# Walsh-Hadamard transform of a ternary feed-forward layer: one butterfly stage moved from VectorE into TensorE's Hadamard products

## The chip, the cores and the metric

The kernel runs as one program on one core of a Trainium2 chip. The metric is the device time of one execution in microseconds (us). In the profile PE is TensorE (PEld its weight loads), DVE is VectorE, ACT is ScalarE, POOL is GpSimd and SP is SyncE, which only issues transfers here. A line such as L1541 is a line of the kernel before.

## The reference, cut to what matters

Two decoder layers of six blocks, each followed by a residual sum and a layer norm, on x of 4 x 512 x 512. Only the third block is touched, a feed-forward block with ternary weights and 8-bit activations, with a Walsh-Hadamard transform ahead of its last product:

```python
def fwht(x):                      # over the last dimension, n = 2048
    h = 1
    while h < n:
        x = x.reshape(-1, n // (2 * h), 2, h)
        a, b = (x[..., 0, :], x[..., 1, :])
        x = jnp.stack([a + b, a - b], axis=-2).reshape(-1, n)
        h *= 2
    return x * (1.0 / np.sqrt(n))

gate = bitlinear(x, w_gate)       # (4, 512, 512) -> (4, 512, 2048)
up = bitlinear(x, w_up)
intermediate = jax.nn.silu(gate) * up
return h_bitlinear(intermediate, w_down)   # act_quant(fwht(.)), then 2048 -> 512
```

The transform of 2048 numbers has eleven stages. Seven act inside blocks of 128 numbers, and are a product with a 128 x 128 matrix of +1 and -1. Four act between the sixteen blocks: distance 1, 2, 4 and 8 blocks.

## The kernel before, in words

The function `ternary_ffn` holds the block. Its work is cut into 16 tiles of 128 rows, and each engine runs its own in-order program, written out by hand as `step(t)` for t from -1 to 15, with semaphores between them. In step t, TensorE makes the gate and up products of tile t in four chunks of 512 columns (`gate_up`, L1511: 8 products of 128x512 bf16 each), turns the rounded transform of tile t-3 (`turn_y`, L1521), turns the butterflied z of tile t-2 (`turn_z`, L1531), multiplies it by the Hadamard matrix (`products`, L1541: four blocks to a PSUM bank, sixteen in all), turns the quantized input of tile t+1 (`turn_q`, L980) and makes the down product of tile t-3 (`down`, L1555). The order is: gate_up 0 and 1, turn_y, turn_z, gate_up 2, products, gate_up 3, turn_q, down. The turned tiles and the products share banks 5 to 7 in rotation; a bank is taken again when ScalarE has copied it out.

VectorE in step t multiplies silu(gate) by up, chunk by chunk (`z_chunk`, L1376, into z), makes three butterfly stages of tile t-1 (`butterfly_stage` 0, 1, 2: distance 2, 4, 8 blocks, each one addition and one subtraction of 128x1024, L1185 and L1186), the quantization of tile t+1, the peaks of |y| of tile t-2 (`peaks`, L1397 to L1406), the residual sum and statistics of tile t-3, and the rounding of y of tile t-2 (`round_y`, L1423). Its order is: z_chunk 0, stage 0, z_chunk 1, stage 1, z_chunk 2, quantized, stage 2, z_chunk 3, peaks, add_down (L1413), statistics, round_y, scale. GpSimd makes the remaining stage, distance 1, from z into z1 (also L1185 and L1186, after the four chunks of z). The stages then go z1 to z2, z2 to z1, z1 to z2, and `turn_z` reads z2.

ScalarE makes the silu (L1276), and copies the turned z (`keep_zT`, L1298), the products (`keep_y`, L1308) and the turned y (`keep_yT`, L1288) out of PSUM. Between peaks and round_y it scales y and adds the rounding constant (`shift_y`, L1314). So the chain of one tile is: products, keep_y, peaks, shift_y, round_y, turn_y, down. In steps 2 and 3 VectorE also rounds the last four chunks of the down weights, and ScalarE copies them to their home (`weights.keep`, L620) ahead of the first `down`.

The Hadamard matrix (`had`, 64 KB) is loaded by SyncE in the stage before. After step 15 the rest of the tiles is worked off: on TensorE turn_y(13), turn_z(14), down(13), products(14), turn_z(15), the first projection of the next block (L92), products(15), turn_y(14), the second projection, down(14), turn_y(15), down(15).

## Time and profile before

| | us |
|---|---|
| median of three runs | 1766.6 |
| lowest and highest run | 1761.59, 1771.72 |
| the profiled execution, whole | 1760.69 |
| its span in the trace | 1758.8 |
| PE busy in the span | 1591.5 |
| DVE busy | 1296.5 |
| ACT busy | 936.4 |
| POOL busy | 690.9 |

A row of groups or of the timeline gives where an instruction starts, how long its record is, and the idle time of its engine before it with the instruction that ended that idle time. A record of a matmul includes its run through the array, which the next one overlaps, so the distance between two starts tells what a matmul costs, and the record does not. The touched block lies between about 504 and 837 us of the span.

### The profile page before, as it was taken

What the parts mean: (1) busy time and instruction counts of PE and PEld (TensorE: products, weight loads), DVE (VectorE), ACT (ScalarE), POOL (GpSimd) and SP (SyncE); (2) the same over time, 40 slices, a digit from 0 to 9 for tenths busy, and PEclk for the clock granted to TensorE, in tenths of its full rate; (3) what the DMA queues carried; (4) which work ended last, traced back from release to release, by engine and by line L of the source; (5) the groups of instructions that cost most, each with busy time, mean ns of one, the idle gap of its engine ahead of it and who ended that gap; (6) DMA issues with size and microseconds to landing.
All of it is one profiled execution on the core that took longest, in us unless ns stands there. A gap on an engine that the chain in (4) does not pass through costs nothing. (4 is left out here: it accounts for less than half of the span.)

```text
span 1758.8 us, 26394 instructions
## 1 busy us (share of the span) xinstructions
PE 1591.5 (90%) x8780; PEld 1121.4 (64%) x8812; DVE 1296.5 (74%) x2354; ACT 936.4 (53%) x1932; POOL 690.9 (39%) x646
## 2 busy tenths in 40 slices
PE   7999998999867899999889999999898989999995
PEld 5788875555525556566666566565566767677774
DVE  6466656666888899997687585784849999767574
ACT  3221226776665566666566465473634555555542
POOL 5034265776522332323332222322132235555553
PEclk9999999999988999999999999999999999999998
DMA  6200018533020000003312121121233100000000
GB/s 213 75 1 24 1 49 234 173 97 97 26 96 1 1 1 1 1 1 104 89 55 73 37 73 55 55 73 37 86 99 93 46 10 1 1 25 12 13 24 24
DMA packets 66849, 95.72 MB, mean 54 GB/s; under 512 B 12176, under 2 KB 28688, under 8 KB 66716
## 3 DMA queue, kind: packets, MB, share of 16 engines
q1 hardware_dynamic: 58460, 80.40, 15.0%
q0 software_dynamic: 6144, 12.60, 2.8%
q8 instruction: 72, 1.18, 0.3%
q10 hardware_dynamic: 2112, 1.05, 0.2%
q14 instruction: 61, 0.50, 0.1%
HBM read 56.25 MB, written 4.19 MB: 34 GB/s over the span
## 5 line engine op out<-in xcount | busy, mean ns | idle before, releaser
L2948 PE MATMUL bank<-fp_xT,fp_weights_values 128*128 128x512 f32 x704 | 187.1, 404 | 11.6 <-DVE fp_gate L2851 9.8
L1783 ACT ACTIVATE causal_probs<-bank,causal_neg 128x512 f32<-128x512 f32 (+3 forms) x256 | 134.1, 530 | 106.0 <-DVE causal_neg L1853 70.8
L2948 PEld LDWEIGHTS bank<-fp_xT,fp_weights_values 128*128 128x128 f32 x704 | 129.7, 190 | 57.1 <-DVE fp_gate L2851 18.0
L2975 PE MATMUL bank<-fp_wd,fp_hT 128*128 128x512 f32 x528 | 133.8, 394 | 4.6 <-DVE X L2873 3.4
L2860 DVE SCALAR_TENSOR_TENSOR fp_up<-bank,fp_weights_scales,fp_up 128x512 f32<-128x512 f32 x132 | 99.1, 751 | 44.5 <-ACT fp_up L2758 37.0
L820 DVE TENSOR_REDUCE heads_neg<-bank 128x1 f32<-128x512 f32 x128 | 86.7, 679 | 57.7 <-PE bank L869 57.6
L782 ACT ACTIVATE heads_probs<-bank,heads_neg 128x512 f32<-128x512 f32 x128 | 88.1, 689 | 77.1 <-DVE heads_neg L820 77.1
L1126 POOL DMA_DIRECT2D causal_qS<-causal_qk x96 | 48.4, 511 | 202.3 <-DVE causal_qk L1118 202.2
L1185 POOL TENSOR_TENSOR ternary_z<-ternary_z 128x1024 f32<-128x1024 f32 x16 | 37.7, 2354 | 206.1 <-DVE ternary_z L1376 206.1
L2975 PEld LDWEIGHTS bank<-fp_wd,fp_hT 128*128 128x128 f32 x528 | 98.5, 188 | 28.9 <-issue 6.6
L1511 PE MATMUL bank<-weights_raw,ternary_qT 128*128 128x512 bf16 x433 | 104.7, 388 | 4.6 <-DVE ternary_z L1376 2.6
L2020 PE MATMUL bank<-eye,causal_probs 128*128 128x128 f32 x640 | 101.8, 283 | 5.2 <-ACT causal_pT L1765 3.7
L92 PE MATMUL bank<-rope_xT,rope_wT 128*128 128x512 f32 x384 | 93.6, 402 | 10.7 <-DVE rope_wT L420 10.7
L2009 PE MATMUL bank<-causal_kS,causal_qS 96*128 96x512 f32 (+3 forms) x256 | 84.5, 382 | 20.0 <-ACT causal_probs L1783 17.2
L330 POOL TENSOR_TENSOR rope_qk<-rope_rot 128x512 f32<-128x512 f32 x32 | 43.0, 1343 | 145.4 <-DVE rope_rot L433 143.9
L80 PE MATMUL bank<-eye,heads_probs 128*128 128x128 f32 x512 | 77.8, 275 | 21.5 <-ACT heads_pT L790 21.4
L2731 POOL TENSOR_TENSOR fp_gate<-fp_gate 128x512 f32<-128x512 f32 x44 | 56.9, 1293 | 100.4 <-DVE fp_gate L2851 100.4
L2752 ACT ACTIVATE fp_gate<-bank,fp_weights_scales 128x512 f32<-128x512 f32 x88 | 60.0, 686 | 62.1 <-PE bank L2948 56.1
L2020 PEld LDWEIGHTS bank<-eye,causal_probs 128*128 128x128 f32 x640 | 78.0, 145 | 22.9 <-issue 12.7
L80 PEld LDWEIGHTS bank<-eye,heads_probs 128*128 128x128 f32 x512 | 59.8, 141 | 51.2 <-ACT heads_probs L782 39.6
L92 PEld LDWEIGHTS bank<-rope_xT,rope_wT 128*128 128x128 f32 x384 | 73.0, 192 | 28.0 <-DVE rope_xT L415 10.7
L2851 DVE SCALAR_TENSOR_TENSOR fp_gate<-bank,fp_weights_scales,fp_gate 128x512 f32<-128x512 f32 x88 | 63.7, 747 | 29.7 <-ACT fp_gate L2752 29.3
(266 smaller groups left out, 4128.2 us busy)
## 6 DMA issues: line engine op xcount, KB each, us to landing
pairs_xd<-X SPq DMA_DIRECT2D x64, 128.0 KB, 2.7
pairs_cd<-in_ctx SPq DMA_DIRECT2D x64, 128.0 KB, 2.8
causal_qS<-causal_qk SPq DMA_DIRECT2D x96, 64.0 KB, 2.8
causal_qS<-causal_qk POOLq DMA_DIRECT2D x96, 64.0 KB, 2.5
causal_kS<-causal_qk SPq DMA_DIRECT2D x96, 64.0 KB, 2.7
causal_kS<-causal_qk POOLq DMA_DIRECT2D x96, 64.0 KB, 2.5
X<-in_x SPq DMA_DIRECT2D x4, 1024.0 KB, 7.8
heads_cT<-in_ctxT SPq DMA_DIRECT2D x4, 1024.0 KB, 6.1
```

Of the source, the lines that this page charges most:

```text
L80: last = pe.transpose(bank[:, k * P:(k + 1) * P], source[:, k, :], ident)
L92: last = pe.matmul(bank, lhs(a, k), rhs(c, k), start=n == 0, stop=n == len(steps) - 1)
L782: act.activation(probs[:, n % 4], banks[n % 3][:], ACT.Exp, bias=neg[:, g % 2, k:k + 1], accum_out=total[:, g % 2, k:k + 1]).then_inc(prob ...
L820: dve.tensor_reduce(neg[:, g % 2, k:k + 1], banks[n % 3][:], AX, ALU.max, negate=True).then_inc(neg_ready, 1)
L1511: last = pe.matmul(to[:], qT[:, t % 2, k], w[c][:, k], start=k == 0, stop=k == NF - 1)
L1783: act.activation(probs_of(i)[:, h + one], view[:, one], ACT.Exp, bias=neg[:, G % 2, at:at + 1], accum_out=total[:, G % 2, at:at + 1]).then ...
L2009: last = pe.matmul(view[:, one], qS[0:3 * DH, G % 2, h + one, i * P:(i + 1) * P], kS[0:3 * DH, G % 2, h + one, 0:(i + 1) * P], start=True, ...
L2020: last = pe.transpose(banks[3 + n % 2][:, h * P:(h + 1) * P], probs_of(i)[:, h, j * P:(j + 1) * P], ident)
L2851: dve.scalar_tensor_tensor(out=part, in0=banks[4 + g][:], scalar=scale(n, g, 0), in1=part, op0=ALU.mult, op1=ALU.add).then_inc(gate_odd, 1)
L2860: dve.scalar_tensor_tensor(out=up[:, n % 2], in0=banks[4 + g][:], scalar=scale(n, g, 1), in1=up[:, n % 2], op0=ALU.mult, op1=ALU.add).then ...
L2948: last = pe.matmul(banks[4 + g][:], values[:, g, n % NI, of], xT[:, part, g], start=part == 0, stop=part == 1)
L2975: last = pe.matmul(banks[t][:], hT[:, n % SLOTS, a, t * P:(t + 1) * P], wd[:, c, i], start=i == 0 and k == 0, stop=i == NI - 1 and k == 2)
```

## The change

The stage of distance 1 leaves the vector engines. TensorE makes it in the Hadamard products: for two neighbouring blocks a and b of the turned z, and the matrix H, the pair of results is [aH + bH, aH - bH]. Where each of the sixteen blocks was multiplied by H alone (128 columns), the first block of a pair is now multiplied by [H, H] (`both`, H read twice) and the second by [H, -H] into the same 256 columns of PSUM, the second accumulating on the first. GpSimd's stage becomes distance 2, VectorE's two stages distance 4 and 8, and its third is gone. The result of the butterflies lies in z1 instead of z2, so `turn_z` reads z1, and GpSimd, which writes z1, waits for `z_turned` of two tiles before in place of the butterflies; VectorE's wait for `z_turned` goes. The matrix in DRAM holds H and -H (128 KB); it has its place in this block, is loaded by SyncE at the block's begin, ahead of the last two loads of weights, and TensorE waits for it ahead of products(0).

```diff
@@ SyncE, stage before
-            start.load_hadamard(sp)
@@ ternary_ffn
+        had = m.sbuf("had", [P, 2, P])
+        both = had[:, 0:1].to_broadcast([P, 2, P])
...
             past.over(sp)
+            sp.dma_start(had[:], hadamard).then_inc(had_loaded, 16)
...
                 pool.wait_ge(z_ready, CH * (t + 1))
                 if t >= 2:
-                    pool.wait_ge(butterfly, 3 * (t - 1))
-                butterflies(pool, z[:, t % 2], z1[:, t % 2], 1).then_inc(first_done, 1)
+                    pool.wait_ge(z_turned, CH * (t - 1))
+                butterflies(pool, z[:, t % 2], z1[:, t % 2], 2).then_inc(first_done, 1)
...
-                src, dst = (z1, z2) if n % 2 == 0 else (z2, z1)
+                src, dst = (z1, z2) if n == 0 else (z2, z1)
                 if n == 0:
                     dve.wait_ge(first_done, t + 1)
-                    if t >= 2:
-                        dve.wait_ge(z_turned, CH * (t - 1))
                 else:
-                    dve.wait_ge(butterfly, 3 * t + n)
-                butterflies(dve, src[:, t % 2], dst[:, t % 2], 2 << n).then_inc(butterfly, 1)
+                    dve.wait_ge(butterfly, 2 * t + 1)
+                butterflies(dve, src[:, t % 2], dst[:, t % 2], 4 << n).then_inc(butterfly, 1)
...
                     quantized(t + 1)
-                butterfly_stage(t - 1, 2)
...
-            for n in range(3):
+            for n in range(2):
                 butterfly_stage(LAST, n)
...
-                    for k in range(4):
-                        last = pe.matmul(to[:, k * P:(k + 1) * P], zT[:, 4 * c + k], had[:], start=True, stop=True)
+                    for k in (0, 2):
+                        pair = to[:, k * P:(k + 2) * P].rearrange("p (two n) -> p two n", two=2)
+                        pe.matmul(pair, zT[:, 4 * c + k], both, start=True, stop=False)
+                        last = pe.matmul(pair, zT[:, 4 * c + k + 1], had[:], start=False, stop=True)
                     last.then_inc(y_ready, 1)
...
-        "hadamard": hadamard(P),
+        "hadamard": np.stack([hadamard(P), -hadamard(P)], axis=1),
```

On TensorE, a step in the middle of the block stands like this before: turn_y (L1521), turn_z (L1531), gate_up 2, the sixteen products, gate_up 3, turn_q, down.

```order
L1521 MATMUL bank<-ternary_eye_2277,ternary_yq 128x128 x16
L1531 MATMUL bank<-eye,ternary_z 128x128 x16
L1511 MATMUL bank<-weights_raw,ternary_qT 128x512 x8
L1541 MATMUL bank<-ternary_had,ternary_zT 128x128 x16
L1511 MATMUL bank<-weights_raw,ternary_qT 128x512 x8
L980 MATMUL bank<-ternary_eye_2277,ternary_q 128x128 x4
L1555 MATMUL bank<-ternary_w_down,ternary_yT 128x512 x16
```

And the same place now, from turn_y (here L1517) to the second pair of products (L1540 the first block of a pair, L1541 the second):

```order
L1517 MATMUL bank<-ternary_eye_2277,ternary_yq 128x128 x16
L1527 MATMUL bank<-eye,ternary_z 128x128 x16
L1507 MATMUL bank<-weights_raw,ternary_qT 128x512 x8
L1540 MATMUL bank<-ternary_had,ternary_zT 128x256
L1541 MATMUL bank<-ternary_had,ternary_zT 128x256
```

There are sixteen products to a tile as before, eight of each line, each of 256 columns instead of 128; nothing else on TensorE has moved.

On VectorE, the middle of a step stands like this before: stage 0 (rows of four runs of 256), a chunk of z, stage 1, a chunk of z, the quantization (L958 to L972), stage 2, the last chunk of z, the peaks.

```order
L1185 TENSOR_TENSOR ternary_z<-ternary_z 128x2x512
L1186 TENSOR_TENSOR ternary_z<-ternary_z 128x2x512
L1376 SCALAR_TENSOR_TENSOR ternary_z<-bank,ternary_steps,ternary_silu 128x512
L958 TENSOR_REDUCE ternary_peak<-X 128x1
...
L972 TENSOR_SCALAR ternary_q<-ternary_q_2273 128x512
L1185 TENSOR_TENSOR ternary_z<-ternary_z 128x1024
L1186 TENSOR_TENSOR ternary_z<-ternary_z 128x1024
L1376 SCALAR_TENSOR_TENSOR ternary_z<-bank,ternary_steps,ternary_silu 128x512
L1397 TENSOR_REDUCE ternary_peak_y<-ternary_y 128x1
```

And now, from the second stage (here the one with runs of 1024) on:

```order
L1183 TENSOR_TENSOR ternary_z<-ternary_z 128x1024
L1184 TENSOR_TENSOR ternary_z<-ternary_z 128x1024
L1375 SCALAR_TENSOR_TENSOR ternary_z<-bank,ternary_steps,ternary_silu 128x512
L952 TENSOR_REDUCE ternary_peak<-X 128x1
...
L966 TENSOR_SCALAR ternary_q<-ternary_q_2273 128x512
L1375 SCALAR_TENSOR_TENSOR ternary_z<-bank,ternary_steps,ternary_silu 128x512
L1394 TENSOR_REDUCE ternary_peak_y<-ternary_y 128x1
```

The pair of butterflies between the quantization and the last chunk of z is gone, and the last chunk follows the quantization directly.

## Rows read from the trace of the kernel before

**Rows 1.** Busy time by stretch: length, PE, PEld, DVE, ACT, POOL, PEclk, DMA

```profile
520.00:560.00 40.00, 25.87 (x139) 16.87 (x140) 33.41 (x50) 22.42 (x32) 9.34 (x4) 0.84 0.00 1
680.00:720.00 40.00, 38.16 (x258) 25.32 (x261) 38.60 (x64) 24.68 (x35) 12.01 (x6) 1.00 0.01 2
```

**Rows 2.** GpSimd's timeline: the same operation in two neighbouring steps

```profile
687.50 2.36 POOL L1185 TENSOR_TENSOR ternary_z<-ternary_z 128x1024 f32<-128x1024 f32 x1 [12.26 <-DVE ternary_z L1376]
705.78 2.35 POOL L1185 TENSOR_TENSOR ternary_z<-ternary_z 128x1024 f32<-128x1024 f32 x1 [12.26 <-DVE ternary_z L1376]
```

**Rows 3.** Timeline of one step, start and length: TensorE from products to turn_y

```profile
717.20 3.73 PE L1541 MATMUL bank<-ternary_had,ternary_zT 128*128 128x128 f32 x32
720.77 1.89 PE L1511 MATMUL bank<-weights_raw,ternary_qT 128*128 128x512 bf16 x8
...
726.17 1.03 PE L1511 MATMUL bank<-weights_first,ternary_qT 128*128 128x512 bf16 x4
727.03 2.75 PE L1511 MATMUL bank<-weights_raw,ternary_qT 128*128 128x512 bf16 x12
730.11 1.07 PE L1521 MATMUL bank<-ternary_eye,ternary_yq 128*128 128x128 bf16 x16 [0.32 <-DVE ternary_yq L1423]
```

**Rows 4.** The same step: VectorE and ScalarE from stage 2 to the rounding

```profile
722.11 1.22 DVE L1186 TENSOR_TENSOR ternary_z<-ternary_z 128x1024 f32<-128x1024 f32 x1
723.25 0.74 DVE L1376 SCALAR_TENSOR_TENSOR ternary_z<-bank,ternary_steps,ternary_silu 128x512 f32<-128x512 f32 x1
726.79 2.00 ACT L1314 ACTIVATE ternary_y<-ternary_y,ternary_rate_y 128x2048 f32<-128x2048 f32 x1 [3.22 <-DVE ternary_rate_y L1406]
728.83 1.23 DVE L1423 TENSOR_SCALAR ternary_yq<-ternary_y 128x2048 bf16<-128x2048 f32 x1
```

**Rows 5.** Groups of instructions, VectorE, 600 to 780 us: busy, mean ns, idle before

```profile
L1186 DVE TENSOR_TENSOR ternary_z<-ternary_z 128x1024 f32<-128x1024 f32 x30 | 36.6, 1219 | 0.0
L1185 DVE TENSOR_TENSOR ternary_z<-ternary_z 128x1024 f32<-128x1024 f32 x30 | 36.5, 1217 | 0.0
```

**Rows 6.** Waits, 600 to 780 us: us in total, times, longest

```profile
PEld bank L1521 <- DVE ternary_yq L1423: 8.6, 10, 1.2
```

**Rows 7.** Groups of f32 matmuls of the next block by width, 840 to 1060 us

```profile
L2040 PE MATMUL bank<-causal_pT,causal_v 128*32 128x256 f32 x56 | 4.3, 379 | 0.0
...
L2080 PE MATMUL bank<-causal_w_o,causal_v_column 128*128 128x512 f32 x8 | 3.6, 592 | 0.0
...
L2040 PE MATMUL bank<-causal_pT,causal_v 128*32 128x128 f32 x56 | 2.8, 273 | 0.0
```

**Rows 8.** Timeline of steps 2 to 4, TensorE and ScalarE's copies of down weights

```profile
539.47 5.45 PE L1541 MATMUL bank<-ternary_had,ternary_zT 128*128 128x128 f32 x32
549.60 1.91 ACT L620 ACTIVATE ternary_w_down<-weights_raw 128x2048 bf16<-128x2048 f32 x1 [0.24 <-DVE weights_raw L615]
556.34 1.89 PE L1521 MATMUL bank<-ternary_eye,ternary_yq 128*128 128x128 bf16 x16 [5.03 <-DVE ternary_yq L1423]
573.28 1.91 ACT L620 ACTIVATE ternary_w_down<-weights_raw 128x2048 bf16<-128x2048 f32 x1 [0.55 <-DVE weights_raw L615]
575.67 4.53 PE L1555 MATMUL bank<-ternary_w_down,ternary_yT 128*128 128x512 bf16 x15 [7.09 <-issue]
583.50 1.06 PE L1521 MATMUL bank<-ternary_eye,ternary_yq 128*128 128x128 bf16 x16
```

**Rows 9.** Timeline of step 15 and the tail

```profile
784.96 1.07 PE L1521 MATMUL bank<-ternary_eye,ternary_yq 128*128 128x128 bf16 x16 [0.33 <-DVE ternary_yq L1423]
795.88 0.75 DVE L1376 SCALAR_TENSOR_TENSOR ternary_z<-bank,ternary_steps,ternary_silu 128x512 f32<-128x512 f32 x1 [1.57 <-ACT ternary_silu L1276]
802.76 1.07 PE L1521 MATMUL bank<-ternary_eye,ternary_yq 128*128 128x128 bf16 x16 [1.64 <-DVE ternary_yq L1423]
819.53 3.73 PE L1541 MATMUL bank<-ternary_had,ternary_zT 128*128 128x128 f32 x32
830.25 1.06 PE L1521 MATMUL bank<-ternary_eye,ternary_yq 128*128 128x128 bf16 x16
```

More of the change, by code:

```diff
@@ L925, with __init__ @@
     QB = 128.0
-    SIZE = 22 * D - 128
-    def __init__(self, nc, names, weights, hadamard, X, banks, ident):
+    def __init__(self, nc, names, weights, X, banks, ident):
         m = self.m = Memory(nc, None, names, "ternary_start")
@@ L931, in __init__ @@
         self.end = self.begin
-        self.weights, self.hadamard, self.X, self.banks, self.ident = weights, hadamard, X, banks, ident
+        self.weights, self.X, self.banks, self.ident = weights, X, banks, ident
         self.q32, self.q, self.qT = (self.place("q32", [P, D], F32, 4 * D), self.place("q", [P, 2, D], BF16, 4 * D),
@@ L935, in __init__ @@
         self.silu = self.place("silu", [P, 2, D], F32, 8 * D)
-        self.eye16, self.had = self.place("eye16", [P, P], BF16, 2 * P), self.place("had", [P, P], F32, 4 * P)
+        self.eye16 = self.place("eye16", [P, P], BF16, 2 * P)
         self.peak, self.step_x, self.rate = (self.place(n, [P, NT], F32, 32) for n in ("peak", "step_x", "rate"))
         self.steps = self.place("steps", [P, NT, 2], F32, 32)
-        self.had_loaded, self.eye_ready = m.sem("had_loaded"), m.sem("eye_ready")
+        self.eye_ready = m.sem("eye_ready")
         self.peaked, self.stepped, self.inverted, self.rated, self.q_shifted, self.q_ready, self.q_turned, self.qT_ready = (
@@ L948, in room @@
         return m.sbuf("start", [P, self.end - self.begin], U8)
-    def load_hadamard(self, sp):
-        sp.dma_start(self.had[:], self.hadamard).then_inc(self.had_loaded, 16)
     def quantized(self, dve, t):
@@ L1018, in __init__ @@
         self.step_in = self.left("step_in", [P, NT - 1, (NT - 1) * GH])
-        self.end = begin + TernaryStart.SIZE
         self.qS, self.kS = self.left("qS", [P, 2, GH, S], F32R), self.left("kS", [P, 2, GH, S], F32R)
@@ L1138, in masked_above, with ternary_ffn @@
         pool.tensor_copy(self.mask[:], ones).then_inc(self.masks, 1)
-def ternary_ffn(nc, block, names, past, start, then, w_ternary, weights, X, norm_tiles, banks, ident):
+def ternary_ffn(nc, block, names, past, start, then, hadamard, w_ternary, weights, X, norm_tiles, banks, ident):
     FF = 4 * D
@@ L1154, in ternary_ffn @@
         start.room(m)
-        had, eye16, qT, silu, steps = start.had, start.eye16, start.qT, start.silu, start.steps
+        eye16, qT, silu, steps = start.eye16, start.qT, start.silu, start.steps
         z = m.sbuf("z", [P, 2, FF])
@@ L1171, in ternary_ffn @@
         down_home = [w_down[:, 4 * c:4 * c + 4].rearrange("p k n -> p (k n)") for c in range(CH)]
+        had_loaded = m.sem("had_loaded")
         q_turned, qT_ready = start.q_turned, start.qT_ready
@@ L1251, in _ @@
                 norm.root(pool, 0, t - 3)
-            pool.wait_ge(butterfly, 3 * TILES)
+            pool.wait_ge(butterfly, 2 * TILES)
             then.kv_lows(pool, 1)
@@ L1526, in turn_z @@
                     return
-                pe.wait_ge(butterfly, 3 * (t + 1))
+                pe.wait_ge(butterfly, 2 * (t + 1))
                 for g in range(CH):
@@ L1530, in turn_z @@
                     for k in range(4):
-                        last = pe.transpose(to[:, k * P:(k + 1) * P], z2[:, t % 2, (4 * g + k) * P:(4 * g + k + 1) * P], ident)
+                        last = pe.transpose(to[:, k * P:(k + 1) * P], z1[:, t % 2, (4 * g + k) * P:(4 * g + k + 1) * P], ident)
                     last.then_inc(z_turned, 1)
@@ L1536, in products @@
                     return
+                if t == 0:
+                    pe.wait_ge(had_loaded, 16)
                 for c in range(CH):
@@ L1578, in step @@
                 down(t - 3)
-            pe.wait_ge(start.had_loaded, 16)
             for t in range(-1, TILES):
@@ L3049, in decoder_kernel @@
                 ternary_names = names()
-                ternary_start = TernaryStart(nc, ternary_names, weights, i["hadamard"], X, banks, ident)
+                ternary_start = TernaryStart(nc, ternary_names, weights, X, banks, ident)
                 heads = head_attention(nc, block, heads_names, rope, pairs, ternary_start, i["ctxT"], i["gamma"], w_ternary, weights, X, norm_tiles[1], banks, ident)
@@ L3055, in decoder_kernel @@
                 causal_start = CausalStart(nc, causal_names, ternary_start.begin, top, gpsimd_copies, i["wqkv"], i["causal_bias"], X, banks, ident)
-                ternary = ternary_ffn(nc, block, ternary_names, heads, ternary_start, causal_start, w_ternary, weights, X, norm_tiles[0], banks, ident)
+                ternary = ternary_ffn(nc, block, ternary_names, heads, ternary_start, causal_start, i["hadamard"], w_ternary, weights, X, norm_tiles[0], banks, ident)
                 heads.names.close()
```

## The prediction, written before the changed kernel was run

> **What bounds the kernel now.** The change touches one block, some 330 of 1759 us, so I read that stretch alone. First the busy times by stretch: in the middle of the block TensorE is busy 38.2 and VectorE 38.6 of 40 us, at a granted clock of 1.00; before that, in the warm-up, neither is, and the clock is 0.84 [rows 1]. Then the period of a step: GpSimd's first butterfly starts at 687.50 and 705.78, so a step takes 18.28 us, with 12.26 us of waiting on GpSimd, which is therefore nobody's bound [rows 2]. Two engines look full, and the question is how much room each has. VectorE's groups show no idle time ahead of the butterflies, and their instructions follow each other at 1.14 us from start to start (722.11 to 723.25) [rows 4, 5]: it has next to none.
>
> For TensorE the busy share says little, since a record holds the run through the array too; I go by starts. From the products at 717.20 to turn_y at 730.11 it has its work back to back, except that the last gate_up record ends at 729.78 and turn_y starts 0.32 us after it, released by the rounding of y [rows 3]. By the weight loads this wait is 8.6 us over 10 steps, 0.86 each [rows 6]. By starts: 12 records of gate_up take 2.75 us and 4 take 1.03, so each costs 0.215, and the last one ends 0.17 us after its share (1.03 - 4 x 0.215) [rows 3]; TensorE could have gone on at 729.61 and lost 0.50 us. That is the wait I use; 0.32 and 0.86 are its bounds. The remaining gaps of a step stand in turn_z, where ScalarE has to empty banks; the change doesn't touch them. So TensorE's own floor is 18.28 - 0.50 = 17.78 us a step: **both engines are full, and TensorE has half a microsecond, not more**.
>
> **What the edit takes from VectorE.** Two instructions of 1.14 us a step, 2.28 us; its work falls to about 16.0 us a step. It is wanted there only if TensorE can follow.
>
> **What it adds to TensorE.** The products are 32 records a tile (each f32 matmul makes two), 3.73 us with one whole record of 0.27 in it: (3.73 - 0.27)/31 = 0.1115 us each [rows 3, 7], 3.57 us in all, which is also the distance to gate_up 3 (717.20 to 720.77) [rows 3]. Now the same 32 have 256 columns. The nearest rows: f32 records of 256 columns last 379 ns and those of 128 columns 273 ns, 106 ns more [rows 7]; and eight f32 records of 512 columns, 0.592 us long, keep TensorE busy for 3.6 us, (3.6 - 0.592)/7 = 0.430 us each, so 0.215 for 256 columns [rows 7]. The first gives 32 x 0.106 = 3.39, the second 32 x 0.215 - 3.57 = 3.31 us more a tile. I take **3.31**; the accumulation on the first block of a pair and the repeated reading of H have no row here, and I give them nothing, with 0 to 0.1 us a tile as bounds.
>
> A rule speaks against such a sum. The Trainium skill ("TensorE: Matmul & The Clock Gate", Back-to-back issue gap) gives sustained 81 ns for a matmul of 128 columns and 131 ns for one of 512. Interpolated, as an estimate, 256 columns would cost 98 ns, 1.2 times those of 128, and the products would add 0.7 us a tile. This trace doesn't agree: 0.1115 and 0.215 us by the rows above. I keep it as a rival with a small chance.
>
> **Whether the wait goes.** TensorE's wait for the rounding of y hangs on the chain products, last chunk of z, peaks, shift, rounding. The last chunk of z began at 723.25, directly behind stage 2, though gate_up 3 had ended at 722.66 [rows 3, 4]. With stage 2 gone it can start at about 722.75, 0.5 us earlier after gate_up 3, and so can peaks, shift_y (726.79 to 728.79) and round_y (728.83 to 730.06). So turn_y would come 9.34 - 0.5 = 8.84 us after gate_up 3 begins, and TensorE's own work ahead of it takes 729.61 - 720.77 = 8.84. They tie: the wait of 0.50 is gone, and nothing more can be had, since TensorE itself is next. A steady step becomes 18.28 + 3.31 - 0.50 = **21.09 us, 2.81 more** (2.45 if all of 0.86 goes, 3.4 if nothing goes and the accumulation costs). VectorE's gain of 2.28 turns into idle time.
>
> **Warm-up.** In steps 2 and 3 TensorE waits 5.03 us for the rounding of y and 7.09 us for the down weights [rows 8], so there the added columns lie beside other work, but not quite: ScalarE makes the silu of the last chunk, which comes after the products, and only then copies down weights. In step 2 the products (539.47, 5.45 us, partly at the lower clock of 1.2 GHz) grow by some 3.4 us, the two copies move behind them, the second from 549.60-551.5 to about 552.8-554.7, and shift and rounding queue behind it: turn_y(0) at 558.0 instead of 556.34, 1.7 late. In step 3 the same happens once more: the last copy, 573.28-575.2, moves to about 576.1-578.0, and down(0), which waits for it, comes 2.8 us late. So turn_y(1), at 583.50, is 2.8 late. If the shorter idle time keeps the higher clock granted, or copies find room, it is 0.8; at worst 3.5.
>
> **Steady part.** From turn_y at 583.50 to 784.96 there are eleven steps (201.5 us) [rows 8, 9]: 11 x 2.81 = 30.9 us (27.0 to 37.4).
>
> **Step 15 and tail.** In step 15 the last chunk of z waits not for VectorE but for ScalarE's silu (1.57 us idle), so VectorE's relief brings nothing and the whole 3.31 reaches turn_y at 802.76. In the tail its two sets of products (819.53 is the second) both stand ahead of turn_y(15) at 830.25, which shows no wait [rows 9]: 6.62. The chain keep_y, peaks, shift, rounding behind the last set moves with it. Together 9.9 (9.3 to 10.3).
>
> **At nothing.** GpSimd's stage has the same 1024 elements an instruction; its new wait for turn_z of two tiles before ends before the fourth chunk of z does, and it has 12.26 us of idle time to cover it. SyncE's load of H, twice as large, is issued at the block's begin, two steps of work ahead of products(0) at 539.47. The memory behind the block moves by 512 bytes a partition.
>
> **Sum.** 2.8 + 30.9 + 9.9 = 43.6 us. On the profiled execution of 1760.7 this gives 1804.3; the median of the runs is 1766.6, 5.9 above it, so I predict 1766.6 + 43.6 = **1810.2 us**, 2.5% slower. By the bounds: 0.8 + 27.0 + 9.3 = 37.1 to 3.5 + 37.4 + 10.3 = 51.2; from the lowest run 1798.7, from the highest 1822.9.
>
> **Rivals.** (a) *The wait stays.* The chain by way of ScalarE gets no shorter, or a new wait (bank rotation of y, the silu behind shift_y) takes its place: 3.31 in each steady step, 11 x 3.31 + 2.8 + 9.9 = 49.1, 1815.7 us. For it: the tie at 8.84 leaves no margin. Against: the last chunk of z does stand directly behind stage 2.
> (b) *TensorE has room, and VectorE's relief is the result.* TensorE's weight loads are busy only 25.3 of 40 us [rows 1]. If that were the measure, 6.7 us a step were free, the 3.31 would vanish in them, and the step would follow VectorE to 16.0 us: 11 x -2.28 = -25, 1741.6 us. It decides where TensorE's floor is under 16.0 - 3.31 = 12.7 us; by the starts it is 17.8. The Trainium skill ("Trainium Kernel Development and Optimization", Performance Expectations) calls matmul busy time a bad metric and the busy share of LDWEIGHTS a good one. Here the first half agrees and the second misleads: loads wait for columns to stream, and the starts show no hole.
> (c) *The columns are mostly hidden,* the pace of 0.1115 being that of the weight loads and not of the 128 columns. Then a tile adds about 0.7 us, a steady step 0.7 - 0.5 = 0.2, and the sum is 11 x 0.2 + 3 x 0.7 + 0.6 = 5 us, 1771.5. Against it: the f32 rows of 128 and 256 columns differ by 106 ns, 128 columns twice over at 2.4 GHz.
>
> **How the numbers follow.** Forecast 0.80, (a) 0.10, (b) 0.05, (c) 0.05. A change under 0.5% (9 us) can hardly be told from none. Faster is (b), 0.05; same is (c), 0.05; slower is the rest, 0.90. The range takes in the forecast's bounds, the spread of the runs and (a): 1797 to 1822; (b) and (c) lie outside.
>
> **What would show it.** Right: GpSimd's first butterflies 21.1 us apart in the middle of the block; 32 records of about 379 ns for the products, 6.9 us to gate_up 3; VectorE busy about 33 of 40 us there with its idle time ahead of the first chunks of z or the add; no more than 0.1 us in TensorE's wait for the rounding; all else in the span as before. Wrong: a period under 20.7 (columns hidden) or over 21.5 (a new wait on TensorE, which would stand ahead of the products or of turn_y), or a block end moved by more or less than the eleven periods tell, which would put the error in the warm-up or the tail.

## The result, and the profile of the changed kernel

The changed kernel took 1806.8 us (median of four runs, 1806.45 to 1809.54) against 1764.4 us of the kernel before on the same chip (also four runs, 1761.59 to 1771.72): a ratio of 1.023, interval 1.0207 to 1.0258. It is slower by 42.4 us; 43.6 were forecast. The span of its profiled execution is 1804.9 us, 46.1 above the 1758.8 of before, at a granted clock of 0.975.

First the busy times by stretch, columns as in [rows 1], one stretch in the warm-up and one in the middle of the block:

```profile
520.00:560.00 40.00, 28.90 (x147) 18.34 (x146) 31.27 (x48) 23.04 (x34) 9.33 (x4) 0.87 0.00 1
...
680.00:720.00 40.00, 39.03 (x224) 25.03 (x223) 30.44 (x51) 21.93 (x32) 12.36 (x6) 1.00 0.00 1
```

In the middle TensorE is now busy 39.03 of 40 us and VectorE 30.44, where [rows 1] had 38.16 and 38.60: one of the two full engines has been relieved, the other is busy almost without a break. The period by GpSimd's timeline, answering [rows 2]:

```profile
683.79 2.35 POOL L1183 TENSOR_TENSOR ternary_z<-ternary_z 128x1024 f32<-128x1024 f32 x1 [14.73 <-DVE ternary_z L1375]
...
704.91 2.35 POOL L1183 TENSOR_TENSOR ternary_z<-ternary_z 128x1024 f32<-128x1024 f32 x1 [14.73 <-DVE ternary_z L1375]
```

704.91 - 683.79 = 21.12 us a step, 18.28 before; GpSimd waits 14.73 us for a tile, 12.26 before. Now TensorE's timeline of a step, answering [rows 3]. The products appear as pairs of records since two lines issue them in turn; the thirteen pairs that follow are left out.

```profile
710.96 1.07 PE L1517 MATMUL bank<-ternary_eye,ternary_yq 128*128 128x128 bf16 x16
...
714.59 1.89 PE L1507 MATMUL bank<-weights_raw,ternary_qT 128*128 128x512 bf16 x8
716.32 0.59 PE L1540 MATMUL bank<-ternary_had,ternary_zT 128*128 128x256 f32 x2
716.75 0.59 PE L1541 MATMUL bank<-ternary_had,ternary_zT 128*128 128x256 f32 x2
717.18 0.59 PE L1540 MATMUL bank<-ternary_had,ternary_zT 128*128 128x256 f32 x2
...
723.22 1.03 PE L1507 MATMUL bank<-weights_raw,ternary_qT 128*128 128x512 bf16 x4
```

Products from 716.32 to gate_up 3 at 723.22: 6.90 us (3.57 in [rows 3]), and turn_y at 710.96 shows no idle time ahead of it. A pair starts every 0.43 us, so each record of 256 columns costs 0.215 us, although it lasts 0.379 by the groups below. The pair that begins a sum (L1540) and the pair that adds to it (L1541) start the next one equally soon, 0.43 us each. VectorE's timeline of the same step, the chunk that comes after the products:

```profile
704.08 0.75 DVE L1375 SCALAR_TENSOR_TENSOR ternary_z<-bank,ternary_steps,ternary_silu 128x512 f32<-128x512 f32 x1 [4.64 <-PE bank L1507]
704.75 2.27 DVE L1394 TENSOR_REDUCE ternary_peak_y<-ternary_y 128x1 f32<-128x2048 f32 x1
...
709.67 1.23 DVE L1420 TENSOR_SCALAR ternary_yq<-ternary_y 128x2048 bf16<-128x2048 f32 x1
```

This is where VectorE's saving went: it stands idle for 4.64 us a step until TensorE has made gate_up 3. Of these, 2.4 come with the longer step, as the first experiment shows, and the rest is the stage that was taken away. The groups and waits over 620 to 800 us (columns as in [rows 5] and [rows 6]) say the same in total:

```profile
L1541 PE MATMUL bank<-ternary_had,ternary_zT 128*128 128x256 f32 x128 | 38.1, 379 | 0.0
```

```profile
DVE ternary_z L1375 <- PE bank L1507: 41.8, 9, 4.7
...
PEld bank L1517 <- DVE ternary_yq L1420: 3.0, 9, 0.3
```

The records are 379 ns long, twice 128 of them in eight steps; VectorE waits 41.8 us for TensorE in nine steps; TensorE's weight loads wait 0.3 us a step for the rounding of y instead of the 0.86 of [rows 6]. Last, the block's ends on TensorE, answering [rows 8] and [rows 9]:

```profile
555.20 1.24 PE L1517 MATMUL bank<-ternary_eye,ternary_yq 128*128 128x128 bf16 x16 [3.33 <-DVE ternary_yq L1420]
```

```profile
574.86 6.06 PE L1555 MATMUL bank<-ternary_w_down,ternary_yT 128*128 128x512 bf16 x16 [4.59 <-issue]
...
584.21 1.06 PE L1517 MATMUL bank<-ternary_eye,ternary_yq 128*128 128x128 bf16 x16
```

```profile
816.57 1.07 PE L1517 MATMUL bank<-ternary_eye,ternary_yq 128*128 128x128 bf16 x16
...
837.70 1.07 PE L1517 MATMUL bank<-ternary_eye,ternary_yq 128*128 128x128 bf16 x16 [1.64 <-DVE ternary_yq L1420]
...
842.99 5.15 PE L1555 MATMUL bank<-ternary_w_down,ternary_yT 128*128 128x512 bf16 x16
```

The landmarks give the account of the span. "Block start" is GpSimd's last sum of the attention stage (497.41 us before, 498.46 after); "first scores" is TensorE's first matmul of the next block's scores (837.53 and 880.90).

| Stretch | before, us | after, us | difference | forecast |
|---|---|---|---|---|
| start to block start (code unchanged) | 497.41 | 498.46 | +1.05 | 0 |
| block start to turn_y at 583.50 / 584.21 | 86.09 | 85.75 | -0.34 | +2.8 |
| eleven steady steps | 201.46 | 232.36 | +30.90 | +30.9 |
| step 15 | 17.80 | 21.13 | +3.33 | +3.31 |
| tail, to the first scores | 34.77 | 43.20 | +8.43 | +6.6 |
| first scores to the end (code unchanged) | 921.3 | 924.0 | +2.7 | 0 |
| span | 1758.8 | 1804.9 | +46.1 | +43.6 |

The rows of the steps fit. The tail is 1.8 us longer than forecast and the warm-up 3.1 shorter. The two stretches of unchanged code vary by themselves: over the profiled executions of before and of the first four experiments below, the last one takes 921 to 928 us.

### The profile page after: what moved, and what is told of

Same layout as the page of the kernel before. It is cut to its first block and busy times, and to the rows that moved or that the text cites. A ratio compares the mean times of both kernels' runs of the same rounds, so it can differ in the third digit from the quotient of the medians.

```text
span 1804.9 us, 26379 instructions
## 1 busy us (share of the span) xinstructions
PE 1649.0 (91%) x8812; PEld 1162.3 (64%) x8812; DVE 1260.8 (70%) x2322; ACT 937.7 (52%) x1932; POOL 692.7 (38%) x646
## 3 DMA queue, kind: packets, MB, share of 16 engines
q10 hardware_dynamic: 2112, 1.05, 0.2%
## 5 line engine op out<-in xcount | busy, mean ns | idle before, releaser
L1375 DVE SCALAR_TENSOR_TENSOR ternary_z<-bank,ternary_steps,ternary_silu 128x512 f32<-128x512 f32 x64 | 47.7, 747 | 67.0 <-PE bank L1507 55.6
```

## Experiments

The theory: a step follows TensorE, whose room was 0.5 us; what 32 records of 256 columns cost more than 32 of 128 is paid in full beyond that, and VectorE's relief is worth only the 0.5 us. The rivals: the relief matters in the steps, or the cost comes from the accumulation or the repeated reading of H and not from the width.

### The width alone

VectorE keeps its three stages and GpSimd the butterfly of neighbouring blocks, as before. Only the products are 256 wide, with a third plane of `had` that makes the added half a zero:

```diff
-        "hadamard": np.stack([hadamard(P), -hadamard(P)], axis=1),
+        "hadamard": np.stack([hadamard(P), 0 * hadamard(P), hadamard(P)], axis=1),
...
-                        pe.matmul(pair, zT[:, 4 * c + k], both, start=True, stop=False)
-                        last = pe.matmul(pair, zT[:, 4 * c + k + 1], had[:], start=False, stop=True)
+                        pe.matmul(pair, zT[:, 4 * c + k], had[:, 0:2], start=True, stop=False)
+                        last = pe.matmul(pair, zT[:, 4 * c + k + 1], had[:, 1:3], start=False, stop=True)
```

> The butterflies are those of the kernel before: GpSimd makes distance 1, VectorE distance 2, 4 and 8. Only TensorE's products change: a pair of blocks is multiplied by [H, 0] and [0, H], each of 256 columns into the same PSUM columns, so the result is the same as before and only the width of the products differs. Theory (TensorE's columns set the step, and VectorE's third stage is hidden as soon as they do): the step goes from 18.28 to 21.1 us as in the changed kernel, because the third stage (ready some 6 us after the products start) is over before gate_up 3 ends (8.7 us after); the whole about 1805 to 1810 us, within 4 us of the changed kernel. Rival (VectorE's relief was worth something in the changed kernel): the step is longer than 21.12 by up to 2.28 us, 21.6 to 23.4, the whole 1813 to 1835 us. Rival (it is the accumulation or the repeated reading of H that costs, not the columns): the repeated reading is gone here, so the step would fall below 21.0.

Measured: 1805.5 us (1803.08 to 1810.43), ratio 1.0235 (1.0208 to 1.0263), the same as the changed kernel. GpSimd's and VectorE's timelines:

```profile
685.05 2.35 POOL L1182 TENSOR_TENSOR ternary_z<-ternary_z 128x1024 f32<-128x1024 f32 x1 [14.73 <-DVE ternary_z L1375]
...
706.18 2.35 POOL L1182 TENSOR_TENSOR ternary_z<-ternary_z 128x1024 f32<-128x1024 f32 x1 [14.73 <-DVE ternary_z L1375]
```

```profile
701.75 1.22 DVE L1183 TENSOR_TENSOR ternary_z<-ternary_z 128x1024 f32<-128x1024 f32 x1
705.35 0.75 DVE L1375 SCALAR_TENSOR_TENSOR ternary_z<-bank,ternary_steps,ternary_silu 128x512 f32<-128x512 f32 x1 [2.39 <-ACT ternary_silu L1275]
```

21.13 us a step with all of VectorE's old work in it, and even so VectorE waits 2.39 us before the last chunk. So in a steady step with wide products VectorE's relief is worth nothing, and reading H twice through a repeated view costs nothing, since this kernel reads it plainly. The accumulation is in this kernel as well; that it costs nothing is told by the starts in the changed kernel, 0.43 us for the pair that begins a sum and for the pair that adds to it. The tail, from turn_y at 838.95 to the first scores at 880.66, takes 41.71 us, 6.94 more than before.

### The relief alone

The changed kernel, but with products of 128 columns, so that the butterfly of neighbouring blocks is left out of the computation:

```diff
-                    for k in (0, 2):
-                        pair = to[:, k * P:(k + 2) * P].rearrange("p (two n) -> p two n", two=2)
-                        pe.matmul(pair, zT[:, 4 * c + k], both, start=True, stop=False)
-                        last = pe.matmul(pair, zT[:, 4 * c + k + 1], had[:], start=False, stop=True)
+                    for k in range(4):
+                        last = pe.matmul(to[:, k * P:(k + 1) * P], zT[:, 4 * c + k], had[:, 0], start=True, stop=True)
```

> The changed kernel with its products brought back to 128 columns each, no pairs: one butterfly stage (distance 1) is left out altogether, so this is VectorE's relief alone without its price on TensorE. Theory: TensorE's own floor of 17.78 us a step shows, 0.50 us less than before, and nothing more of the 2.28 us taken from VectorE; 11 steps give -5.5 us, the warm-up perhaps 1 to 3 us less, the whole 1755 to 1761 us. Rival (VectorE sets the step and TensorE has room): 16.0 us a step, the whole 1737 to 1742 us.

Measured: 1752.4 us (1748.47 to 1755.63), ratio 0.9926 (0.9903 to 0.9949). GpSimd's timeline:

```profile
681.34 2.36 POOL L1183 TENSOR_TENSOR ternary_z<-ternary_z 128x1024 f32<-128x1024 f32 x1 [11.39 <-DVE ternary_z L1375]
...
699.13 2.36 POOL L1183 TENSOR_TENSOR ternary_z<-ternary_z 128x1024 f32<-128x1024 f32 x1 [11.40 <-DVE ternary_z L1375]
```

17.79 us a step: taking two instructions of 1.14 us from VectorE gains 0.49, which is the wait of 0.50 that the prediction read off, and TensorE's floor stands at the 17.78 that it named: VectorE now waits 1.3 us a step for gate_up 3 (11.8 us in nine steps). The run also shows what the prediction had not counted: the warm-up (block start 498.87 to turn_y 580.68) takes 81.8 us, 4.3 less than before.

### Half of the width

As the first experiment, but only two of a tile's four banks are made 256 wide:

```diff
-                    for k in range(4) if c not in (0, 1, 2, 3) else ():
+                    for k in range(4) if c not in (0, 2) else ():
```

> As the kernel with wide products and the butterflies of before, but only two of the four banks of products are made wide (256 columns), the other two keep four products of 128 columns; the result is the same. Theory (cost goes with columns, 0.83 us a bank, over TensorE's floor of 17.78): 17.78 + 1.66 = 19.4 us a step, if the third stage on VectorE is hidden; if VectorE's stage still stands ahead of the last chunk of z, up to 19.9. Rival (a fixed cost of pairs, or a new wait that comes with wide products at all): the same 21.1 as with all four banks wide, or the whole extra at once.

Measured in a single run: 1778.7 us, and by GpSimd's timeline 695.03 to 714.48, 19.45 us a step:

```profile
695.03 2.35 POOL L1182 TENSOR_TENSOR ternary_z<-ternary_z 128x1024 f32<-128x1024 f32 x1 [13.06 <-DVE ternary_z L1375]
...
714.48 2.35 POOL L1182 TENSOR_TENSOR ternary_z<-ternary_z 128x1024 f32<-128x1024 f32 x1 [13.06 <-DVE ternary_z L1375]
```

17.79, 19.45, 21.12 for no, two and four wide banks: 0.83 us a bank, the same both times. Neither the first two wide banks nor the last two are free; one bank alone was not measured. And with VectorE's three stages kept, the step of 19.45 still lies on this line, so between 18.28 and 19.45 TensorE has already taken over as the bound.

### Can the half microsecond be had in another way?

The relief was worth 0.49 us a step as long as TensorE doesn't pay for it. GpSimd has 12 us of idle time, so it makes the second stage (distance 2) too, and VectorE two stages, behind its quantization:

```diff
                 butterflies(pool, z[:, t % 2], z1[:, t % 2], 1).then_inc(first_done, 1)
...
+                butterflies(pool, z1[:, t % 2], z2[:, t % 2], 2).then_inc(first_done, 1)
```

> The kernel before, with the stage of distance 2 moved from VectorE to GpSimd, which waits 12.26 us of each step: GpSimd makes z to z1 (distance 1), the root of the norm, then z1 to z2 (distance 2); VectorE makes distance 4 and 8, after the quantization and after the third chunk of z; the products keep 128 columns. Theory: VectorE loses its 2.28 us at no price on TensorE, so the step is TensorE's floor, 17.8 us, as in the kernel with the relief alone; -5.5 us in the steady part, the whole 1755 to 1762 us, 0.3 to 0.6% faster than before. Rival (VectorE slows down while GpSimd works, or the two stages of GpSimd at 2.35 us an instruction become the chain): no gain, 1764 us or more, with waits of VectorE for GpSimd in each step.

Measured: 1764.4 us (1758.79 to 1768.47, twelve runs), ratio 0.9996 (0.9981 to 1.0011): no difference. The step alternates between 17.87 and 18.41 us. Its VectorE, group and timeline, and its GpSimd at the same time:

```profile
L206 DVE TENSOR_SCALAR X<-X,norm_mean_var,norm_rstd 128x512 f32<-128x512 f32 x9 | 22.5, 2505 | 2.5 <-POOL norm_rstd L199 2.2
```

```profile
676.34 1.23 DVE L1427 TENSOR_SCALAR ternary_yq<-ternary_y 128x2048 bf16<-128x2048 f32 x1
677.63 2.42 DVE L206 TENSOR_SCALAR X<-X,norm_mean_var,norm_rstd 128x512 f32<-128x512 f32 x1
679.97 1.40 DVE L1382 SCALAR_TENSOR_TENSOR ternary_z<-bank,ternary_steps,ternary_silu 128x512 f32<-128x512 f32 x2
```

```profile
676.78 2.98 POOL L1185 TENSOR_TENSOR ternary_z<-ternary_z 128x1024 f32<-128x1024 f32 x1
679.72 2.56 POOL L1186 TENSOR_TENSOR ternary_z<-ternary_z 128x1024 f32<-128x1024 f32 x1
```

The normalisation (L206), 0.55 us in the changed kernel, lasts 2.42 us when it begins while GpSimd adds: it ends 0.3 us after GpSimd's instruction of 676.78 has ended (680.05 and 679.76). VectorE saved 2.28 us and lost 1.9 of it.

So the normalisation was moved, by one tile, behind the quantization:

```diff
                     quantized(t + 1)
+                norm.scale(dve, 0, t - 4)
...
                 round_y(t - 2)
-                norm.scale(dve, 0, t - 3)
```

> As the kernel with two stages on GpSimd, but VectorE's normalisation of tile t-3 (L206), which took 2.42 to 2.57 us there beside GpSimd's second stage instead of 0.55, is made one step later, after the quantization, when GpSimd is idle. Theory (that kernel lost its gain only because this one instruction stood still while GpSimd worked): the instruction takes 0.55 us again, VectorE has about 16 us of work a step, and every step is 17.8 us instead of 17.9 and 18.4 in turn; the warm-up stays as slow as there (turn_y of tile 1 at about 586.5). Rival (GpSimd's second stage slows VectorE's other instructions as well): the step stays over 18.0 us.

Measured in a single run: 1762.4 us, 17.97 us a step. VectorE's groups:

```profile
L963 DVE TENSOR_SCALAR ternary_steps<-weights_mean,ternary_step_x 128x2 f32<-128x2 f32 x9 | 21.1, 2349 | 0.0
```

L206 is back at 0.54 us, but the next `tensor_scalar` in line, one of two elements a partition that took 0.21 us, now takes 2.35. The stall belongs to the time, not to the instruction; of the 0.49 us, 0.31 are gained in a step (18.28 - 17.97).

Both kernels also lose in the warm-up: from block start to turn_y of tile 1 they take 88.8 and 88.2 us instead of 86.1. To see whether that is GpSimd's second stage, the first three tiles leave it with VectorE:

```diff
+        BY_POOL = 3
+        by_pool = lambda t: t >= BY_POOL
```

> As the kernel with the normalisation moved, but the first three tiles keep their three stages on VectorE, so that nothing of GpSimd's second stage falls into the warm-up, where VectorE rounds weights. Theory: turn_y of tile 1 comes at 583.5 as in the kernel before, then eleven steps of 17.8 us: -5.4 us against before, the whole 1756 to 1760 us (0.3% faster). Rival: the warm-up was not slow because of GpSimd, turn_y of tile 1 stays at 586 or later, the whole 1761 us or more.

Measured: 1761.5 us (1760.1 to 1763.2, ten runs), ratio 0.9985 (0.9971 to 0.9999), steps of 17.97, turn_y at 586.13, where 583.5 had been expected. From block start these are 88.3 us, so most of the lost time is still there without GpSimd's second stage. It stands in one place, the down product of tile 0. In this version, then in the kernel before, where it starts at 575.67 [rows 8]:

```profile
576.34 6.50 PE L1574 MATMUL bank<-ternary_w_down,ternary_yT 128*128 128x512 bf16 x16 [6.71 <-issue]
...
582.68 1.03 PE L1530 MATMUL bank<-weights_first,ternary_qT 128*128 128x512 bf16 x4
```

```profile
580.04 1.03 PE L1511 MATMUL bank<-weights_first,ternary_qT 128*128 128x512 bf16 x4
```

From its start to the next gate_up it takes 6.34 us here, at a granted clock of 0.55; in the kernel before, with the same code up to this place, it takes 4.37 us at 0.75, after idle times of much the same length (6.71 and 7.09 us). That is 2.0 of the 2.2 us. In the two versions ahead of this one the same product takes 5.9 us, 1.5 of the 2.7 and 2.1 us lost there; only the rest can belong to GpSimd's second stage. So a part of the warm-up differs from execution to execution, and a single profile can't place turn_y there to 2 us. The timelines show the stall beside GpSimd at its plainest:

```profile
678.09 0.15 DVE L960 TENSOR_SCALAR ternary_step_x<-ternary_peak 128x1 f32<-128x1 f32 x1
678.27 0.16 DVE L962 RECIPROCAL ternary_peak<-ternary_step_x 128x1 f32<-128x1 f32 x1
678.35 2.35 DVE L963 TENSOR_SCALAR ternary_steps<-weights_mean,ternary_step_x 128x2 f32<-128x2 f32 x1
680.61 0.14 DVE L965 TENSOR_SCALAR ternary_rate<-ternary_peak 128x1 f32<-128x1 f32 x1
```

```profile
678.32 2.35 POOL L1186 TENSOR_TENSOR ternary_z<-ternary_z 128x1024 f32<-128x1024 f32 x1
```

L963 and GpSimd's instruction end together, at 678.35 + 2.35 = 680.70 and 678.32 + 2.35 = 680.67.

With VectorE relieved, TensorE's own waits in turn_z are next. They could vanish if z is turned first and y behind it, since ScalarE would then have emptied the banks of y:

```diff
-                turn_y(t - 3)
                 turn_z(t - 2)
+                turn_y(t - 3)
```

> As the kernel with GpSimd's second stage from tile 3 on, and TensorE turns z of tile t-2 ahead of y of tile t-3 in each step (ScalarE copies in that order too). Theory (TensorE's floor of 17.79 us holds some 0.9 us of waiting in turn_z for ScalarE's copies of the turned y at 1.02 us a bank, and the chain to turn_y has 0.5 us of margin where it comes after turn_z): turning z first needs only copies of 0.52 us, and what waits for them is shorter; the step falls to 17.0 to 17.3 us, the whole 1748 to 1754 us, about 0.7% faster than before. Rival (ScalarE is still in shift_y and the silus when turn_z begins, and the wait only moves): 17.8 us, 1757 us.

Measured: 1759.8 us (1758.57 to 1763.37, twelve runs), ratio 0.9977 (0.9964 to 0.9990). By the medians it is the fastest version of this study that computes everything, but its interval overlaps with those of the version ahead of it and of the last one below, and the steady step stays at 17.98 instead of the 17.0 to 17.3 expected. Its waits over 620 to 780 us:

```profile
PEld bank L1550 <- ACT ternary_zT L1309: 9.3, 8, 1.5
PE bank L1550 <- ACT ternary_zT L1309: 7.4, 8, 1.2
```

The wait has moved: turn_z of the fourth bank now waits for ScalarE's copy out of the first, 0.9 us a time. What gain there is lies ahead of the steady part. Turning in step 4 begins at 583.01 (with z) instead of 586.13 (with y), and 1.4 of these 3.1 us are again the down product of tile 0, 4.98 us instead of 6.34. The period behind it is 16.91 us instead of 18.17. Against that, the stretch from the turning in step 15 to the first scores is 2.5 us longer (55.2 instead of 52.6), 1.5 us of it in down(13), which took 5.07 us here at a granted clock of 0.71. So no gain from the order of turning is shown.

The stall beside GpSimd remained in this version. To be rid of it, GpSimd's second stage waits for the rounding of y, and VectorE gets other work in that place, the addition of the down product and its statistics, with the quantization behind them; the normalisation moves behind VectorE's last stage:

```diff
                 if by_pool(t):
+                    pool.wait_ge(yq_ready, t - 1)
...
                 if late:
+                    add_down(t - 4)
+                    norm.statistics(dve, 0, t - 4)
                     quantized(t + 1)
```

> As the kernel with GpSimd's second stage from tile 3 on, but laid so that no f32 tensor_scalar of VectorE falls beside GpSimd: GpSimd begins its second stage only after round_y (a wait on yq_ready), VectorE makes the residual sum and statistics of tile t-4 after the second chunk of z, ahead of the quantization, and the normalisation after its last stage. Theory (an f32 tensor_scalar of VectorE stands still until GpSimd's running instruction ends: 2.3 us a step, which moved from the normalisation to the first tensor_scalar of the quantization when only the normalisation was moved): the step falls from 17.97 to TensorE's floor of 17.79 us, L963 takes about 0.2 us or waits at most 0.6 us, the whole 1758 to 1761 us. Rival: the collision finds another instruction, step 17.9 to 18.3.

Measured: 1763.1 us (1760.9 to 1765.71, ten runs), ratio 0.9993 (0.9981 to 1.0005), 18.21 us a step. VectorE's groups:

```profile
L1436 DVE TENSOR_SCALAR ternary_yq<-ternary_y 128x2048 bf16<-128x2048 f32 x9 | 11.0, 1227 | 18.6 <-ACT ternary_y L1325 18.6
...
L963 DVE TENSOR_SCALAR ternary_steps<-weights_mean,ternary_step_x 128x2 f32<-128x2 f32 x9 | 5.6, 627 | 0.0
```

The collision is mostly gone (0.63 us instead of 2.12), and a wait of the same size stands elsewhere: VectorE now waits 18.6 / 9 = 2.1 us a step for ScalarE's shift of y ahead of the rounding. The addition and the statistics had been filling just that hole. Together with z turned first (the same swap as above) it was expected to show TensorE's shorter floor:

> As the kernel without collisions, with TensorE turning z ahead of y as well. Theory (turning z first gained nothing in the steps because ScalarE was still in shift_y and the silus, which came late since VectorE stood still 2.3 us ahead of the last chunk of z): the peaks and shift_y come about 2 us earlier, ScalarE is free when z is turned, and the step falls to 17.0 to 17.3 us; the whole 1749 to 1754 us. Rival (the bank rotation waits for ScalarE in any order): 17.8 us, the whole 1757 to 1760 us.

Measured: 1760.9 us (1756.36 to 1765.54, twelve runs), ratio 0.9981 (0.9968 to 0.9994), still 18.21 us a step instead of 17.0 to 17.3. VectorE has the same wait of 2.1 us for the shift, which itself waits for VectorE's peaks, and no other of size, so VectorE's own chain sets the period, and TensorE's order has nothing to give.

## Why the prediction was right, and where it was not

**The steady step** is right in both of its terms. The width was put at 3.31 us by the f32 records of 512 columns [rows 7]; from the second experiment to the changed kernel it is 21.12 - 17.79 = 3.33, and the third shows it linear. The other bound, 106 ns a record by the difference of durations, would have given 3.39. The pace is read from the starts: 0.215 us from record to record, where the records are 0.379 long. TensorE's floor was put at 17.78 and is 17.79; the wait for the rounding of y has gone, as the chain's 0.5 us by way of VectorE said. Forecast 21.09, measured 21.12.

**The middle of the block,** eleven steps, came to +30.90 as forecast, and **step 15** to +3.33 against 3.31: with the width alone it takes 21.12 us, so there VectorE's relief brings nothing, as the silu's wait in [rows 9] told.

**The tail** was put at 6.62 and is 6.94 with the width alone. In the changed kernel's profiled execution it is 8.43; of this, down(13) accounts for 1.53, since its sixteen records took 5.15 us at 842.99 and 3.62 us in every steady step. The stretch was run at a lower granted clock, 0.70 in this row of the busy times by stretch (columns as in [rows 1]). down(13) took 3.62 us in the experiments with the width alone and with the relief alone, and 5.07 us in the version that turns z first, whose products have 128 columns. So it is neither half of the edit by itself; what lowers the clock there in some executions is not shown:

```profile
843.00:848.20 5.20, 5.20 (x19) 2.27 (x18) 1.84 (x3) 0.83 (x2) 0.00 (x0) 0.70 0.14 40
```

**The warm-up** is the term that was mis-sized: +2.8 forecast, -0.34 measured. The step that failed is the first one: the products of step 2 were to grow by some 3.4 us and push ScalarE's copies of down weights back, and behind them shift, rounding and turn_y(0), by 1.7 us, and step 3 was to add the rest. Two things stood against it. First, VectorE's relief is worth most here. In the kernel before, the last chunk of z of step 2 came at 549.48, behind a butterfly (543.03) and four instructions that round the weights (544.56 to 549.57). The chunk before, then after, and ScalarE after:

```profile
549.48 0.74 DVE L1376 SCALAR_TENSOR_TENSOR ternary_z<-bank,ternary_steps,ternary_silu 128x512 f32<-128x512 f32 x1
```

```profile
547.37 0.75 DVE L1375 SCALAR_TENSOR_TENSOR ternary_z<-bank,ternary_steps,ternary_silu 128x512 f32<-128x512 f32 x1 [1.16 <-PE bank L1507]
```

```profile
548.09 3.90 ACT L620 ACTIVATE ternary_w_down<-weights_raw 128x2048 bf16<-128x2048 f32 x2
551.90 1.99 ACT L1313 ACTIVATE ternary_y<-ternary_y,ternary_rate_y 128x2048 f32<-128x2048 f32 x1
```

The chunk comes 2.1 us earlier, although in this execution the block itself began 1.05 us later. The second copy no longer waits for its weights, and turn_y follows at 555.20, 1.1 us before that of [rows 8]; counted from block start these are 3.2 and 2.2 us. Second, the products. TensorE's timeline of before, then of after, then of the width alone:

```profile
539.23 0.38 PE L1566 MATMUL bank<-weights_sums,weights_ones 128*128 128x1 f32 x2 [3.28 <-DVE weights_sums L600]
```

```profile
538.15 0.38 PE L1566 MATMUL bank<-weights_sums,weights_ones 128*128 128x1 f32 x2 [0.54 <-DVE weights_sums L600]
538.40 0.68 PE L1540 MATMUL bank<-ternary_had,ternary_zT 128*128 128x256 f32 x2
```

```profile
540.90 0.38 PE L1571 MATMUL bank<-weights_sums,weights_ones 128*128 128x1 f32 x2 [2.84 <-DVE weights_sums L600]
```

TensorE waits 0.54 us for VectorE's sums ahead of the products where it waited 3.28, and starts the products 1.07 earlier than in [rows 8], 2.1 counted from block start. With the width but without the relief the same matmul comes at 540.90, and the block began at 498.95, so there it is as late as before. The busy times of the products' stretch, after and before, have the granted clock near their end:

```profile
538.40:545.40 7.00, 7.00 (x35) 6.08 (x35) 6.72 (x14) 1.79 (x3) 0.00 (x0) 1.00 0.00 0
```

```profile
539.50:544.90 5.40, 5.40 (x34) 5.34 (x35) 5.19 (x13) 1.79 (x3) 0.00 (x0) 0.68 0.00 0
```

It is 1.00 after, the upper level of 2.4 GHz throughout, and 0.68 before, a part of the stretch at 1.2 GHz. So twice the columns took 6.99 us, from 538.40 to 545.39, against 5.28 to gate_up's start before: they grew by 1.7 us and not by 3.4. A clock held up was in the prediction, as its bound of 0.8; the relief was not. The experiments put sizes on both. All times but the last row's count from block start (497.41, 498.95, 498.87 and 498.46 us):

| | before | width alone | relief alone | both |
|---|---|---|---|---|
| last chunk of z, step 2 | 52.07 | 52.19 | 48.34 | 48.91 |
| turn_y of tile 0 | 58.93 | 59.06 | 55.20 | 56.74 |
| down of tile 0 | 78.26 | 78.03 | 72.38 | 76.40 |
| turn_y of tile 1 | 86.09 | 86.56 | 81.81 | 85.75 |
| down of tile 0 to the next gate_up | 4.37 | 5.07 | 5.97 | 5.90 |

The width alone makes nothing late up to the down product: the products take 6.99 us at a granted clock of 1.00, as in the changed kernel, and from turn_y of tile 0 to the products of step 3 it takes 5.36 us at 1.00, where the kernel before took 6.56 at 0.65. The relief alone brings the down product 5.9 us forward, and the width takes 4.0 of it back. VectorE is the later of the two there, until it is relieved; the prediction had put the width on the path and the relief off it.

The down product itself is the same code in all four, and its granted clock was, in the order of the table, 0.75, 0.68, 0.58 and 0.59; so up to 1.6 us of the differences in turn_y of tile 1 come from that clock. Each kernel was profiled once. The medians of all runs agree with the picture: 42.4 us slower with both, 42.6 with the width alone, 10.5 faster with the relief alone (against 1762.8 us of the kernel before, 17 runs, in the last two). Whether the clock of 1.00 in the products is due to the edits or to the execution stays open: with half of the width it was 0.72.

**The sum** came out 1.2 us above the medians' difference and 2.5 below the profiled executions', closer than its parts, and that is luck: the warm-up's 3.1 us too much stands against 1.8 too little in the tail and 3.8 us by which the unchanged code was longer in this execution. The time itself was forecast at 1810.2 and measured at 1806.8; 2.2 of the 3.4 us are the median of before, 1766.6 from three runs and 1764.4 from the four here. **VectorE's busy time** of "about 33 of 40" was wrong by its own numbers: 16.0 us of work in 21.1 is 30.3 of 40, and 30.4 is measured.

**The rivals.** (a) *The wait stays*: no, the step would be 21.6. (b) *TensorE has room*: its floor would have to lie under 12.7 us and the step with relief alone at 16.0; it is 17.79. The busy time of the weight loads is of no use for it: 25.3 of 40 us in [rows 1], when TensorE had 0.50 us of room in a step, and 25.0 now that it has 0.02 (twelve records of gate_up from 708.36 at 0.215 us end at 710.94, and turn_y starts at 710.96). The Trainium skill ("Trainium Kernel Development and Optimization", Performance Expectations) names that share, beside the share of peak arithmetic, as a good measure of how close a kernel is to its limit. Here it stands at 63% both times, with the engine full but for 3% of a step and then full. (c) *The columns are mostly hidden*: no, by 0.83 us a bank.

## What to carry to other kernels

Where two engines are full, moving work from one to the other gains only the wait between them, and costs all that it adds beyond that wait, in each stretch by itself: 0.49 us a step in the steady part here, some 4 us once in the warm-up, where the relieved engine was late. So read the receiving engine's room from the starts of its instructions between two waits, not from a busy share. An f32 product made twice as wide to fold an addition in costs its columns in full on a TensorE that has no gap (3.33 us here for two VectorE instructions of 1.14). And where the engine that receives work is idle, look first at what it shares with the engine that is to be relieved.

## What the runs showed of the hardware

A VectorE `tensor_scalar` from memory to memory stood still here while a GpSimd `tensor_tensor` ran. The normalisation of 512 elements took 2.42 us instead of 0.55, and a `tensor_scalar` of two elements 2.35 instead of 0.21, until the GpSimd instruction had ended (680.70 and 680.67 in the second case); when one was moved away, the next took its place. It went the other way too: the same GpSimd instruction took 2.98 us instead of 2.35 when it began at 676.78 beside the rounding of y (676.34, 1.23 us), also a `tensor_scalar`. Not held up in the same stretches were `tensor_reduce` (0.67 us for 512 elements at 677.38 beside GpSimd in the version where GpSimd starts late, 0.68 us in the kernel before at 539.74, with GpSimd idle), the `scalar_tensor_tensor` that reads a bank (0.70 us each) and `tensor_scalar` of a single element (0.15 us). The Trainium skill ("SBUF — State Buffer", SBUF: two separate sides) states such a rule: the two engines share a pair of ports as an exclusive lock, and whichever starts first, GpSimd or a VectorE instruction that uses the pair, holds it for the whole of its instruction. It counts among the VectorE instructions those in a mode that uses both ports, and those with two inputs in SBUF. The trace agrees in both directions for `tensor_scalar`; VectorE's butterflies, which have two inputs, did not run beside GpSimd in the stretches shown. So the idle 12.26 us of GpSimd in [rows 2] were not free to use. How much of the missing 0.18 us a step (0.31 gained of 0.49) is due to the stall is not shown, since the version in which it was mostly gone had a step of 18.21 us for another reason.

The cost of the products' width is even over the measured points, none, two and four wide banks: 0.83 us for each bank of four 128-column blocks that became 256 wide. With four wide banks it is the same with and without VectorE's third stage (21.13 and 21.12 us a step).
